# Moving the keys' trailing subtraction of the rotated rows from VectorE to Pool

## The chip, the cores and the metric

One core of one Trainium2 chip runs the whole program: a decoder layer in float32. The time is device microseconds (us) of one launch. Engines: PE is TensorE, DVE is VectorE, ACT is ScalarE, POOL is GpSimd (called Pool in the text), SP is SyncE, which only issues DMAs here.

## The reference

The input x is 4 sequences of 1024 rows of 256 numbers. The layer is self-attention with 16 heads of 16, cross-attention over 77 rows of context, and a mixture of 8 experts. The change touches the projection of the self-attention only:

```python
qkv = x @ qkv_w.T + qkv_b          # x is the layernorm of the input
q = q * cos + x_rot(q) * sin       # apply_rotary
k = k * cos + x_rot(k) * sin
attn = softmax(einsum('bhqd,bhkd->bhqk', q, k) * scale)
```

## The kernel before

The program runs in stages: the projection (`project_qkv`, 0 to some 104 us of the trace), the attention (`attend`), cross-attention and experts.

**Chunks.** The projection takes the 4096 rows in J = 8 chunks of 512, c = 0 to 7; two chunks are one sequence. For each chunk the rows are normalised, transposed, and multiplied by the weights. Products are made of a leading and a trailing part of each float32 number, so that three passes of TensorE give the precision.

**Pairs.** The queries of chunk c are pair n = 2c, the keys are pair n = 2c + 1. One pair goes through these steps, each on one engine:

- TensorE `pair(n)` (L416, L419) multiplies into two banks.
- VectorE `rotate(n)` (L331, twice) multiplies them by the tables into `a_by_even` and `a_by_odd`. It waits until Pool has summed pair n - 2, whose buffers it overwrites.
- Pool (L392) adds the two into `a_rotated`, which has one half for queries and one for keys. Here this is called sum n.
- ScalarE `split(n)` (L263) copies the sum into `a_parts` as the leading part.
- VectorE `split(n)` (L339) subtracts the leading part from the sum; this is the trailing part. Here it is called subtraction n.
- SyncE `store_pair(n)` (L164) stores the parts to `q_stacks` or `k_stacks` with 4 DMAs.

The last three pairs (13, 14, 15) have their subtractions in the next stage, on Pool (`end_sums`, L174 to L180).

**The rest of VectorE's list.** In chunk c it runs `rotate(2c)`, `trailing(c + 1)` (L319, the trailing part of the transposed rows, read from PSUM), `moments(c + 3)` (L302, L305), subtraction 2c - 1, in chunks 0, 2 and 4 `spread(c + 2, 2)`, then `rotate(2c + 1)` and subtraction 2c. `spread` makes one over the standard deviation of the next two chunks in 13 tiny instructions that wait for each other: three TENSOR_SCALAR (L312, L60, L61), nine of Newton's steps (L67, L68, L69) and L314. ScalarE can only normalise chunks c + 2 and c + 3 (L237, `a_xn`) behind it, and TensorE transposes them (L404) behind that.

**The other orders.** ScalarE's list in chunk c is: copy of the values (L254), `take(c + 1)` (L245), leading parts 2c - 1 and 2c, copy of the values, their store (L156), `normalise(c + 2)`. Pool's list is the sums in order, with two memsets (L471, `b_k`, the padding of the first group) between sum 2 and sum 3. SyncE's list is the stores in order of pairs; behind the store of pair 7 and of pair 9 it issues the loads of `b_q` and `b_k` (L483) for the first group of heads, behind the store of pair 11 that of `b_v` (L486), and then the store of pair 12. All the engines meet at a barrier between the projection and the attention.

**The start of the attention.** TensorE's first products there (L879) are for the row maxima; they wait for all of the first group (`pe.wait_ge(s_ld[0], LD)`). VectorE reduces each (L811). The maxima of the first rows go by DMA into `b_q` (L677). The first scores (L930) wait for that, and with them the main loop, which TensorE and VectorE fill. Pool, behind the barrier, does `end_sums`, clears the padding of group 1 and issues its loads; SyncE stores the last three pairs.

Of the kernel before, what the change touches and what calls it, by code (L numbers as in the profile page):

```python
# [8 lines left out]
F32 = mybir.dt.float32  # L9
# [85 lines left out]
def project_qkv(nc, ps, ident, s_id, group0, s_clear0, stores, tail, s_end, cw, x, wts, qst, kst, vst):  # L95
# [5 lines left out]
    with ctx:  # L101
        sb = lambda n, s, d=F32: ctx.enter_context(nc.sbuf_tensor(n, s, d))
        sem = lambda n: ctx.enter_context(nc.semaphore(n))
        J = 2 * B
# [33 lines left out]
        s_eo = sem("a_rotated")  # L138
# [7 lines left out]
        def after(eng, s, n):  # L146

            if n > 0:
                eng.wait_ge(s, n)

        def half(c):
            return slice(CH * (c % 2), CH * (c % 2) + CH)

        def store_v(sp, c):
            i, h = c // 2, c % 2
            sp.dma_start(vst[i][:, NT * h:NT * h + NT, :],  # L156
                         vsb[:, h].rearrange("p t h d -> p t (h d)")).then_inc(s_vs[h], 16)
# [43 lines left out]
        @block.sync  # L201
        def _(sp):
            load(sp, 0)
            sp.dma_start(w, wts["wqkv"]).then_inc(s_w, 16)
            sp.dma_start(ident[:], wts["ident"]).then_inc(s_id, 16)
            load(sp, 1)
            sp.dma_start(bias[:], wts["bqk"]).then_inc(s_tab[0], 16)
            load_tables(sp, 0)
            load(sp, 2)
            load(sp, 3)  # L210
            load_tables(sp, 1)
            sp.dma_start(cw["wp"][:], wts["wp"].rearrange("(k p) n -> p k n", p=P)).then_inc(s_wp, 16)
            sp.dma_start(cw["bp"][:], wts["bp"].partition_broadcast(P)).then_inc(s_wp, 16)
            sp.dma_start(bv[:], wts["bvqkv"]).then_inc(s_wp, 16)
            for c in range(J - 1):
                sp.wait_ge(s_pb, 2 * c + 1)
                store_pair(sp, 2 * c)
                if c == J - 2:
                    continue
                sp.wait_ge(s_pb, 2 * c + 2)  # L220
                store_pair(sp, 2 * c + 1)
                if c == J - 5:
                    for h in range(2):
                        sp.wait_ge(s_vs[h], 16)
                        sp.wait_ge(s_qs[h], 128)
                    sp.wait_ge(s_clear0, 4)
                if J - 5 <= c < J - 2:
                    load_group(sp, *group0, qst, kst, vst, 0, 0, part=c - J + 5)

        @block.scalar  # L230
        def _(act):
            def normalise(c):
                h = c % 2
                act.wait_ge(s_stat, c + 1 if c < 2 else 2 + c // 2)
                after(act, s_xT, c - 1)
                for t in range(NT):
                    last = nc.scalar.activation(xn[:, h, t, :], xin[:, c % NX, t, :], ACT.Identity,  # L237
                                                bias=nm[:, c % NX, t:t + 1], scale=rs[:, c % NX, t:t + 1])
                last.then_inc(s_xn, 1)

            def take(c):
                act.wait_ge(s_xT, c + 1)
                after(act, s_vp, 2 * c - 2)
                for k in range(KC):
                    last = nc.scalar.activation(xh[:, c % 2, k, :], ps[:, k, :], ACT.Copy)  # L245
                last.then_inc(s_xh, 1)

            def copy_v(m):
                c, u = m // 2, m % 2
                act.wait_ge(s_vp, m + 1)  # L250
                if u == 0:
                    act.wait_ge(s_v0, 1)
                    after(act, s_vs[c % 2], 16 * (c // 2))
                nc.scalar.activation(vsb[:, c % 2, 2 * u:2 * u + 2, :, 0:D],  # L254
                                     ps[:, 6 + u, :].rearrange("p (t h d) -> p t h d", t=2, d=D), ACT.Copy).then_inc(s_vc, 1)

            def split(n):
                c, s = n // 2, n % 2
                act.wait_ge(s_eo, n + 1)
                if s == 0:  # L260
                    after(act, s_qs[c % 2], 128 * (c // 2))
                summed = whole(n, 1).bitcast(F32) if n == 2 * J - 3 else eo[:, n % 2]
                nc.scalar.activation(whole(n, 0), summed, ACT.Copy).then_inc(s_pa, 1)  # L263

            def refill(c):
                if c < J:
                    act.wait_ge(s_xn, c - NX + 1)
                    load(act, c)

            act.wait_ge(s_w, 16)  # L270
            nc.scalar.activation(wh[:], w, ACT.Copy).then_inc(s_wh, 1)
            normalise(0)
            refill(NX)
            take(0)
            normalise(1)
            refill(NX + 1)
            for c in range(J):
                copy_v(2 * c)
                if c + 1 < J:
                    take(c + 1)  # L280
                if c:
                    split(2 * c - 1)
                if c < J - 1:
                    split(2 * c)
                copy_v(2 * c + 1)
                act.wait_ge(s_vc, 2 * c + 2)
                store_v(act, c)
                if c + 2 < J:
                    normalise(c + 2)
                    refill(c + 2 + NX)  # L290

        @block.vector
        def _(dve):
# [27 lines left out]

            def rotate(n):
                q, at = n % 2, half(n // 2)
                after(dve, s_eo, n - 1)
                if n == 2 * J - 1:
                    by = last_even[:], last_sum[:]
                else:
                    by = by_even[:, q], by_odd[:, q]
                for u, s in ((0, s_ev), (1, s_od)):
                    dve.wait_ge(s, n + 1)  # L330
                    last = v.scalar_tensor_tensor(by[u], ps[:, 2 + 2 * q + u, :].unsqueeze(1).to_broadcast([P, 2, CH]),  # L331
                                                  bias[:, 2 * q + u:2 * q + u + 1], tab[:, 2 * u:2 * u + 2, at],
                                                  ALU.add, ALU.mult)
                last.then_inc(s_t, 1)

            def split(n):
                c, s = n // 2, n % 2
                dve.wait_ge(s_pa, n + 1)
                v.tensor_tensor(whole(n, 1), eo[:, n % 2], whole(n, 0).bitcast(F32), ALU.subtract).then_inc(s_pb, 1)  # L339

# [8 lines left out]
            for c in range(J):  # L349
# [6 lines left out]
                    trailing(c + 1)  # L356
                if c and c + 3 < J:
                    moments(c + 3)
                if 0 < c < J - 1:
                    split(2 * c - 1)  # L360
                if c % 2 == 0 and c + 2 < J:
                    spread(c + 2, 2)
                if c == 3:
# [11 lines left out]
        def _(pool):  # L375
            g = nc.gpsimd
            clear_pad(g, pool, group0[0], s_clear0, 0)
            for n in range(2 * J - 1):
                q = n % 2
                after(pool, s_eo, n)  # L380
                if n == 3:
                    clear_pad(g, pool, group0[1], s_clear0, 2)
                pool.wait_ge(s_t, n + 1)
                after(pool, s_pb, n - 1)
                if n == 2 * J - 2:
                    to = sum_before[:]
                elif n == 2 * J - 3:
# [2 lines left out]
                else:  # L390
                    to = eo[:, q]
                g.tensor_tensor(to, by_even[:, q], by_odd[:, q], ALU.add).then_inc(s_eo, 1)  # L392

        @block.tensor
        def _(pe):
# [1708 lines left out]
```

## Time and profile before

| what | value |
|---|---|
| median of 3 runs | 1180.93 us (1179.43 to 1181.35) |
| the profiled execution, its own time | 1183.38 us |
| its span in the trace | 1181.6 us |
| busy PE, DVE, ACT, POOL | 92%, 86%, 65%, 30% of the span |
| projection | 0 to some 104 us |
| first maximum product, first score of the attention | 104.00 us, 137.43 us |

Busy time says how long an engine had work, and not who was waited for. So the questions are put to the stretch of the projection and the start of the attention alone: who idles there, and what ends each wait. Times below are from the start of the span.

### The profile page before, as it was taken

What the parts mean: (1) busy time and instruction counts of PE and PEld (TensorE: products, weight loads), DVE (VectorE), ACT (ScalarE), POOL (GpSimd) and SP (SyncE); (2) the same over time, 40 slices, a digit from 0 to 9 for tenths busy, and PEclk for the clock granted to TensorE, in tenths of its full rate; (3) what the DMA queues carried; (4) which work ended last, traced back from release to release, by engine and by line L of the source; (5) the groups of instructions that cost most, each with busy time, mean ns of one, the idle gap of its engine ahead of it and who ended that gap; (6) DMA issues with size and microseconds to landing.
All of it is one profiled execution on the core that took longest, in us unless ns stands there. A gap on an engine that the chain in (4) does not pass through costs nothing. (4 is left out here: it accounts for less than half of the span.)

```text
span 1181.6 us, 22857 instructions
## 1 busy us (share of the span) xinstructions
PE 1082.7 (92%) x8540; PEld 596.6 (50%) x8540; DVE 1014.3 (86%) x2168; ACT 767.8 (65%) x932; POOL 352.3 (30%) x316
## 2 busy tenths in 40 slices
PE   7989899999999999999999999999984059999998
PEld 6776333333333333333333333347773048888897
DVE  7998799999999999999999999716998975766663
ACT  4552288788888888888887888864565014655653
POOL 2647822202220221122022000022100022765675
PEclk8987599999999999999999999999997559999999
DMA  7787844514422441443144000036532022554443
GB/s 232 258 252 220 199 74 90 97 23 80 75 52 44 80 78 27 69 79 67 24 84 75 20 12 17 17 105 212 178 107 94 0 72 60 152 147 125 111 112 36
DMA packets 84681, 113.95 MB, mean 96 GB/s; under 512 B 25056, under 2 KB 57568, under 8 KB 84576
## 3 DMA queue, kind: packets, MB, share of 16 engines
q1 hardware_dynamic: 66256, 69.82, 20.0%
q0 software_dynamic: 15024, 36.17, 17.0%
q10 hardware_dynamic: 3296, 6.56, 1.6%
q8 instruction: 65, 1.06, 0.4%
q14 instruction: 40, 0.33, 0.1%
HBM read 73.31 MB, written 38.27 MB: 94 GB/s over the span
## 5 line engine op out<-in xcount | busy, mean ns | idle before, releaser
L811 DVE TENSOR_REDUCE b_max_halves<-banks 128x1 f32<-128x512 f32 x1024 | 626.5, 681 | 13.1 <-PE banks L879 12.9
L748 ACT ACTIVATE b_probs<-banks 128x1024 f32<-128x1024 f32 x512 | 520.4, 1026 | 145.3 <-PE banks L930 145.3
L879 PE MATMUL banks<-b_k,b_q 62*128 62x512 f32 x1024 | 398.4, 469 | 6.0 <-PEq L101 1.5
L930 PE MATMUL banks<-b_q,b_k 64*128 64x512 f32 x1024 | 385.6, 456 | 4.5 <-issue 3.3
L901 PE MATMUL banks<-b_probs,b_v 128*17 128x256 f32 (+1 forms) x3840 | 314.8, 400 | 0.2 <-ACT b_probs L748 0.2
L930 PEld LDWEIGHTS banks<-b_q,b_k 64*128 64x128 f32 x1024 | 157.0, 185 | 224.5 <-issue 170.8
L879 PEld LDWEIGHTS banks<-b_k,b_q 62*128 62x128 f32 x1024 | 161.9, 190 | 40.3 <-DVE b_max_halves L811 38.0
L901 PEld LDWEIGHTS banks<-b_probs,b_v 128*17 128x17 f32 x3840 | 63.9, 95 | 165.1 <-issue 98.5
L551 POOL TENSOR_TENSOR b_att<-b_out,b_rec_spread 128x512 f32<-128x512 f32 x32 | 41.1, 1283 | 310.9 <-DMA b_rec_spread<-reciprocals 310.7
L483 POOL DMA_DIRECT2D b_q<-q_stacks x60 | 31.7, 532 | 226.4 <-PE banks L901 214.3
L1850 DVE TENSOR_TENSOR e_hTl<-e_hT,e_hTh 128x512 fp32r<-128x512 f32 x64 | 47.6, 744 | 48.8 <-ACT e_hT L1604 48.8
L1630 POOL DMA_INDIRECT e_x<-rows,d_idx x32 | 45.3, 1414 | 111.0 <-DVE d_wx L1805 57.5
L1601 ACT ACTIVATE e_hTh<-banks,e_b 128x512 fp32r<-128x512 f32 x64 | 44.1, 689 | 52.5 <-PE banks L1962 49.0
L1962 PE MATMUL banks<-e_w2h,e_hTh 128*128 128x256 f32 x256 | 73.1, 286 | 0.0
L1962 PE MATMUL banks<-e_w2l,e_hTh 128*128 128x256 f32 x256 | 72.4, 283 | 0.0
L1962 PE MATMUL banks<-e_w2h,e_hTl 128*128 128x256 f32 x256 | 72.4, 283 | 0.0
L1587 ACT ACTIVATE e_xTh<-banks 128x512 fp32r<-128x512 f32 x16 | 8.7, 596 | 83.3 <-PE banks L1950 83.3
L1653 POOL DMA_INDIRECT out_x<-c_x,d_idx x32 | 55.3, 1728 | 17.7 <-DVE c_x L1883 11.0
L1962 PE MATMUL banks<-e_xTh,e_w1h 128*128 128x512 f32 x128 | 53.9, 421 | 3.2 <-DVE e_xTl L1818 2.6
L1962 PE MATMUL banks<-e_xTl,e_w1h 128*128 128x512 f32 x128 | 51.2, 400 | 0.0
L1962 PE MATMUL banks<-e_xTh,e_w1l 128*128 128x512 f32 x128 | 50.9, 397 | 0.0
L392 POOL TENSOR_TENSOR a_rotated<-a_by_even,a_by_odd 128x1024 f32<-128x1024 f32 x13 | 36.4, 2802 | 47.2 <-DVE a_by_odd L331 46.8
(259 smaller groups left out, 1476.5 us busy)
## 6 DMA issues: line engine op xcount, KB each, us to landing
e_w<-in_w SPq DMA_DIRECT2D x16, 1024.0 KB
q_stacks<-a_parts SPq DMA_DIRECT2D x32, 256.0 KB, 4.2
k_stacks<-a_parts SPq DMA_DIRECT2D x32, 256.0 KB, 4.1
b_q<-q_stacks POOLq DMA_DIRECT2D x30, 256.0 KB, 6.4
b_k<-k_stacks POOLq DMA_DIRECT2D x30, 256.0 KB, 7.2
v_tiles<-a_v ACTq DMA_DIRECT2D x8, 544.0 KB, 3.7
b_rec_spread<-reciprocals SPq DMA_DIRECT2D x128, 32.0 KB, 1.8
attended<-b_att SPq DMA_DIRECT2D x128, 32.0 KB, 2.6
```

The source lines that it names most:

```text
L392: g.tensor_tensor(to, by_even[:, q], by_odd[:, q], ALU.add).then_inc(s_eo, 1)
L551: g.tensor_tensor(self.att[:, x, :], self.osb[:, x, :], self.rb[:, x, :], ALU.mult).then_inc(self.s_att, 1)
L748: nc.scalar.activation(pr[:, S % NP, u], ps[:, 2 * u:2 * u + 2, :], ACT.Exp, scale=D ** -0.5).then_inc(s_ex[u], 1)
L811: v.tensor_reduce(mxp[:, (k // NB) % 2, s, p, t, kh:kh + 1], ps[:, bank(last), :], AX.X, ALU.max)\
L879: nc.tensor.matmul(ps[:, bank(last), :], qs[g][stack, p, at:at + P], ks[g][stack, p, CH * kh:CH * kh + CH], start=True, stop=True).then_in ...
L901: last = nc.tensor.matmul(ps[VW * j:VW * j + VS, PV, at], vs[hg // 2][:, kt, j, :], pr[:, S % NP, j // 2, j % 2, at], start=(kt == 0), sto ...
L930: return nc.tensor.matmul(ps[:, 2 * u + s, :], ks[g][stack, u, P * kt:P * kt + P], qs[g][stack, u, CH * h:CH * h + CH], start=True, stop=True)
L1601: nc.scalar.activation(hh[:, f, :], ps[:, UP[f % len(UP)], :], ACT.Gelu, bias=b1[:, x, f:f + 1])
L1630: g.indirect_dma_start(xe[:, x, h, :], None, xrow, bass.IndirectOffsetOnAxis(ap=idx[:, n, h:h + 1], axis=0))\
L1653: g.indirect_dma_start(out, bass.IndirectOffsetOnAxis(ap=idx[:, n, h:h + 1], axis=0), y[:, h, :], None, compute_op=ALU.add).then_inc(s_sc, 16)
L1850: v.tensor_tensor(hl[:, f, :], hf[:, f % NH, :], hh[:, f, :], ALU.subtract).then_inc(s_hl, 1)
L1962: ins = mm(o, a, b, start=(start and m == 0), stop=(stop and m == len(pairs) - 1))
```

## The change

The keys' subtractions 1, 3, 5, 7, 9 and 11 leave VectorE's list. Pool does each of them behind the sum of the pair that follows: sum 2, subtraction 1, (the memsets), sum 3, sum 4, subtraction 3, and so on. Both operands and the result are the same tiles as before. The queries' subtractions 0, 2, ... 12 stay on VectorE. As Pool's semaphore `s_eo` now counts sums and subtractions, the helper `added(n)` tells its value behind sum n and `parted(n)` its value behind subtraction n; the waits of SyncE, ScalarE and VectorE are rewritten for that.

```diff
@@ -151,6 +151,12 @@
         def half(c):
             return slice(CH * (c % 2), CH * (c % 2) + CH)
 
+        def added(n):
+            return n + 1 + max(0, n // 2 - (n % 2 == 0))
+
+        def parted(n):
+            return added(n + 1) + 1
+
         def store_v(sp, c):
             i, h = c // 2, c % 2
             sp.dma_start(vst[i][:, NT * h:NT * h + NT, :],
@@ -213,11 +219,11 @@
             sp.dma_start(cw["bp"][:], wts["bp"].partition_broadcast(P)).then_inc(s_wp, 16)
             sp.dma_start(bv[:], wts["bvqkv"]).then_inc(s_wp, 16)
             for c in range(J - 1):
-                sp.wait_ge(s_pb, 2 * c + 1)
+                sp.wait_ge(s_pb, c + 1)
                 store_pair(sp, 2 * c)
                 if c == J - 2:
                     continue
-                sp.wait_ge(s_pb, 2 * c + 2)
+                sp.wait_ge(s_eo, parted(2 * c + 1))
                 store_pair(sp, 2 * c + 1)
                 if c == J - 5:
                     for h in range(2):
@@ -256,7 +262,7 @@
 
             def split(n):
                 c, s = n // 2, n % 2
-                act.wait_ge(s_eo, n + 1)
+                act.wait_ge(s_eo, added(n))
                 if s == 0:
                     after(act, s_qs[c % 2], 128 * (c // 2))
                 summed = whole(n, 1).bitcast(F32) if n == 2 * J - 3 else eo[:, n % 2]
@@ -321,7 +327,8 @@
 
             def rotate(n):
                 q, at = n % 2, half(n // 2)
-                after(dve, s_eo, n - 1)
+                if n > 1:
+                    dve.wait_ge(s_eo, added(n - 2))
                 if n == 2 * J - 1:
                     by = last_even[:], last_sum[:]
                 else:
@@ -334,7 +341,6 @@
                 last.then_inc(s_t, 1)
 
             def split(n):
-                c, s = n // 2, n % 2
                 dve.wait_ge(s_pa, n + 1)
                 v.tensor_tensor(whole(n, 1), eo[:, n % 2], whole(n, 0).bitcast(F32), ALU.subtract).then_inc(s_pb, 1)
 
@@ -356,8 +362,6 @@
                     trailing(c + 1)
                 if c and c + 3 < J:
                     moments(c + 3)
-                if 0 < c < J - 1:
-                    split(2 * c - 1)
                 if c % 2 == 0 and c + 2 < J:
                     spread(c + 2, 2)
                 if c == 3:
@@ -377,11 +381,13 @@
             clear_pad(g, pool, group0[0], s_clear0, 0)
             for n in range(2 * J - 1):
                 q = n % 2
-                after(pool, s_eo, n)
+                if n:
+                    pool.wait_ge(s_eo, added(n) - 1)
                 if n == 3:
                     clear_pad(g, pool, group0[1], s_clear0, 2)
                 pool.wait_ge(s_t, n + 1)
-                after(pool, s_pb, n - 1)
+                if n > 1 and q == 0:
+                    pool.wait_ge(s_pb, n // 2)
                 if n == 2 * J - 2:
                     to = sum_before[:]
                 elif n == 2 * J - 3:
@@ -390,6 +396,10 @@
                 else:
                     to = eo[:, q]
                 g.tensor_tensor(to, by_even[:, q], by_odd[:, q], ALU.add).then_inc(s_eo, 1)
+                if q == 0 and 0 < n < 2 * J - 2:
+                    pool.wait_ge(s_pa, n)
+                    pool.wait_ge(s_eo, added(n))
+                    g.tensor_tensor(whole(n - 1, 1), eo[:, 1], whole(n - 1, 0).bitcast(F32), ALU.subtract).then_inc(s_eo, 1)
 
         @block.tensor
         def _(pe):
```

Pool's list, from sum 2 to sum 5. Before:

```order
L392 TENSOR_TENSOR a_rotated<-a_by_even,a_by_odd 128x1024 [waits a_trailing_part,a_parts_of_rotation_ready,a_rotated]
L471 MEMSET b_k 32x2048 [waits a_rotated]
L471 MEMSET b_k 32x2048 [waits group0_pad_cleared]
L392 TENSOR_TENSOR a_rotated<-a_by_even,a_by_odd 128x1024 [waits a_trailing_part,a_parts_of_rotation_ready,group0_pad_cleared]
L392 TENSOR_TENSOR a_rotated<-a_by_even,a_by_odd 128x1024 [waits a_trailing_part,a_parts_of_rotation_ready,a_rotated] x9
```

With the change:

```order
L398 TENSOR_TENSOR a_rotated<-a_by_even,a_by_odd 128x1024 [waits a_trailing_part,a_parts_of_rotation_ready,a_rotated]
L402 TENSOR_TENSOR a_parts<-a_rotated,a_parts 128x2x512 [waits a_rotated,a_leading_part]
L481 MEMSET b_k 32x2048 [waits a_rotated]
L481 MEMSET b_k 32x2048 [waits group0_pad_cleared]
L398 TENSOR_TENSOR a_rotated<-a_by_even,a_by_odd 128x1024 [waits a_parts_of_rotation_ready,group0_pad_cleared]
L398 TENSOR_TENSOR a_rotated<-a_by_even,a_by_odd 128x1024 [waits a_trailing_part,a_parts_of_rotation_ready,a_rotated]
L402 TENSOR_TENSOR a_parts<-a_rotated,a_parts 128x2x512 [waits a_rotated,a_leading_part]
L398 TENSOR_TENSOR a_rotated<-a_by_even,a_by_odd 128x1024 [waits a_parts_of_rotation_ready,a_rotated]
```

A subtraction (now L402) stands behind every sum of queries, and the one in front of the memsets is ahead of sum 3.

VectorE's list in chunk 2, from the rotation of its queries to the first instructions of `spread`. Before:

```order
L331 SCALAR_TENSOR_TENSOR a_by_even<-banks,a_bias,a_cos_sin 128x1024
L331 SCALAR_TENSOR_TENSOR a_by_odd<-banks,a_bias,a_cos_sin 128x1024
L319 TENSOR_TENSOR a_xnT_trailing<-banks,a_xnT_leading 128x512 x2
L302 BN_STATS a_st<-a_x 128x6 x4
L305 BN_AGGR a_mv<-a_st 128x2 x4
L339 TENSOR_TENSOR a_parts<-a_rotated,a_parts 128x2x512
L312 TENSOR_SCALAR a_ve<-a_mv 128x8
L60 TENSOR_SCALAR a_tm<-a_ve 128x8
```

With the change:

```order
L338 SCALAR_TENSOR_TENSOR a_by_even<-banks,a_bias,a_cos_sin 128x1024
L338 SCALAR_TENSOR_TENSOR a_by_odd<-banks,a_bias,a_cos_sin 128x1024
L325 TENSOR_TENSOR a_xnT_trailing<-banks,a_xnT_leading 128x512 x2
L308 BN_STATS a_st<-a_x 128x6 x4
L311 BN_AGGR a_mv<-a_st 128x2 x4
L318 TENSOR_SCALAR a_ve<-a_mv 128x8
L60 TENSOR_SCALAR a_tm<-a_ve 128x8
```

The subtraction between the moments and `spread` is gone; nothing else moved on this engine.

## Rows read from the trace of the kernel before

**Rows 1.** Windows of 10 us: each engine's busy time (x instructions), PEclk, DMA share, GB/s.

```profile
70.00:80.00 10.00, 7.09 (x33) 6.08 (x33) 9.56 (x21) 5.28 (x10) 3.40 (x2) 0.75 0.82 226
...
80.00:90.00 10.00, 10.00 (x57) 8.77 (x56) 9.22 (x8) 5.95 (x10) 6.14 (x3) 0.91 0.96 282
...
90.00:100.00 10.00, 10.00 (x56) 8.69 (x55) 9.09 (x10) 4.29 (x6) 6.14 (x3) 1.00 1.03 286
```

**Rows 2.** Timeline of VectorE, chunks 2 to 5 (start us, us, instruction, idle before).

```profile
50.67 0.17 DVE L314 SCALAR_TENSOR_TENSOR a_nm<-a_mv,a_rs 128x8 f32<-128x8 f32 x1
...
64.65 1.28 DVE L331 SCALAR_TENSOR_TENSOR a_by_even<-banks,a_bias,a_cos_sin 128x1024 f32<-128x1024 f32 x1
...
70.07 1.23 DVE L339 TENSOR_TENSOR a_parts<-a_rotated,a_parts 128x1024 fp32r<-128x1024 f32 x1
...
71.21 0.17 DVE L312 TENSOR_SCALAR a_ve<-a_mv 128x8 f32<-128x8 f32 x1
...
71.82 0.17 DVE L67 SCALAR_TENSOR_TENSOR a_tm<-a_rs,a_ve 128x8 f32<-128x8 f32 x1
...
73.63 0.17 DVE L314 SCALAR_TENSOR_TENSOR a_nm<-a_mv,a_rs 128x8 f32<-128x8 f32 x1
...
80.82 2.49 DVE L339 TENSOR_TENSOR a_parts<-a_rotated,a_parts 128x1024 fp32r<-128x1024 f32 x1
```

**Rows 3.** Timeline of Pool, the same columns.

```profile
36.67 3.68 POOL L471 MEMSET b_k<- 32x2048 f32 x2
...
44.28 2.42 POOL L392 TENSOR_TENSOR a_rotated<-a_by_even,a_by_odd 128x1024 f32<-128x1024 f32 x1 [0.26 <-DVE a_by_odd L331]
...
67.25 2.42 POOL L392 TENSOR_TENSOR a_rotated<-a_by_even,a_by_odd 128x1024 f32<-128x1024 f32 x1 [0.25 <-DVE a_by_odd L331]
...
79.85 2.38 POOL L392 TENSOR_TENSOR a_rotated<-a_by_even,a_by_odd 128x1024 f32<-128x1024 f32 x1 [0.28 <-DVE a_by_odd L331]
...
103.96 0.52 POOL L763 MEMSET b_minus<- 2x512 f32 x1 [2.67 <-POOLq L101]
...
106.97 2.36 POOL L176 TENSOR_TENSOR a_parts<-a_parts 128x1024 fp32r<-128x1024 f32 x1
```

**Rows 4.** Timeline of a later stage: a sum on Pool, small instructions of VectorE.

```profile
833.48 2.35 POOL L1178 TENSOR_TENSOR c_xb<-c_x,c_bp 128x1024 f32<-128x1024 f32 x1 [9.82 <-DMA c_x<-in_x]
...
835.23 0.70 DVE L1283 SCALAR_TENSOR_TENSOR c_ve<-c_mv,c_eps 128x4 f32<-128x4 f32 x2
```

**Rows 5.** Timeline of TensorE, and of VectorE's last maxima ahead of the first score.

```profile
53.00 1.09 PE L404 MATMUL banks<-ident,a_xn 128*128 128x128 f32 x8 [2.65 <-ACT a_xn L237]
...
75.95 1.97 PE L404 MATMUL banks<-ident,a_xn 128*128 128x128 f32 x8 [2.91 <-ACT a_xn L237]
...
104.00 0.70 PE L879 MATMUL banks<-b_k,b_q 62*128 62x512 f32 x3 [1.45 <-PEq L101]
...
125.46 9.66 DVE L811 TENSOR_REDUCE b_max_halves<-banks 128x1 f32<-128x512 f32 x16
...
137.43 0.76 PE L930 MATMUL banks<-b_q,b_k 64*128 64x512 f32 x1 [3.26 <-issue]
```

**Rows 6.** Timeline of DMA issues: SyncE's queue, then ScalarE's last one.

```profile
83.34 2.45 SPq L164 DMA_DIRECT2D k_stacks<-a_parts  x4
...
96.67 0.88 SPq L486 DMA_DIRECT2D b_v<-v_tiles  x1
...
97.59 4.89 SPq L164 DMA_DIRECT2D q_stacks<-a_parts  x4
...
103.21 0.33 ACTq L156 DMA_DIRECT2D v_tiles<-a_v  x1
```

**Rows 7.** Waits from 83 to 108 us: who waited, for whom, us in total, times, longest.

```profile
PEld banks L879 <- DMA b_v<-v_tiles: 1.6, 1, 1.6
```

**Rows 8.** Windows of 2 us, columns as in the first group.

```profile
84.00:86.00 2.00, 2.00 (x10) 1.64 (x9) 2.00 (x3) 1.52 (x3) 0.17 (x1) 1.00 0.83 252
...
130.00:132.00 2.00, 2.00 (x4) 0.94 (x4) 2.00 (x4) 0.00 (x0) 1.94 (x2) 0.50 1.04 175
```

## The prediction

> **What bounds the kernel now.** The chain of the page covers only the end of the program, so I read the windows first. In the projection VectorE is busy 9.56 and 9.22 us of 10, while TensorE is at 7.09 once, with its clock on 0.75, that is half of that stretch at 1.2 and half at 2.4 GHz [rows 1]. So VectorE paces this stage, and an engine with room, Pool (3.40 and 6.14 us of 10), takes work from it. That speaks for a gain. The reader should then see three things against it. TensorE waits 2.65 and 2.91 us for the normalised rows before the transposes of chunks 4 and 6 [rows 5]; these wait for `spread`, which ends on VectorE at 50.84 and 73.80 [rows 2]. The DMA share is 0.96 and 1.03 from 80 to 100 us [rows 1]: the DMAs are full. And at the end TensorE does not start the attention when it has finished; its weight loads wait 1.6 us for the DMA of `b_v` [rows 7], the first product runs at 104.00 [rows 5].
>
> **Does Pool hold VectorE up?** Sum 10 runs on Pool from 79.85 to 82.23 [rows 3], and the subtraction that VectorE begins at 80.82 beside it takes 2.49 us instead of 1.23 [rows 2]. In a later stage even tiny ones wait: two 128x4 instructions (L1283) take 0.70 us when they begin at 835.23 beside a sum of Pool that ends at 835.83, and end 0.1 us behind it [rows 4]; an instruction of that size takes 0.17 [rows 2]. Both kinds read two operands in SBUF, and Pool reads there too. L67, L68, L69 and L314 in `spread` are of that kind. Rotations, `trailing` and moments are not (their inputs are one in PSUM, or one alone), so I let them run.
>
> **The change, step by step.** Six subtractions leave VectorE. An undisturbed one holds it 71.21 - 70.07 = 1.14 us [rows 2], number 9 holds it 2.42. Read as busy time that is 5 x 1.14 + 2.42 = 8.1 us (number 11 taken as undisturbed). Pool gains six of 2.36 us [rows 3]; I lay them into its list and go through the chunks.
>
> - Chunk 1: subtraction 1 is gone, VectorE is 1.14 ahead.
> - Chunk 2: a second 1.14 is gone, but Pool is late. Sum 2 ended at 36.62, and the memsets took its place at 36.67 for 3.68 us [rows 3]. Now subtraction 1 runs first, to 39.05, the memsets to 42.8, sum 3 to 45.25, sum 4 to 47.7 (it began at 44.28 before and is 1.0 later), subtraction 3 to 50.1. `spread` takes 1.81 us from L67 at 71.82 to L314 at 73.63, nine steps of 0.2 [rows 2]; so L67 stood at 50.67 - 1.81 = 48.86 here and would now stand 2.28 earlier, at 46.6. It waits for sum 4 until 47.7, its second step for subtraction 3 until 50.1. Eight steps of 0.2 and the 0.17 of L314 follow. That ends at 51.85 against 50.84: **1.0 us later**. TensorE's wait of 2.65 becomes 3.7.
> - Chunk 3: no `spread`, 1.14 ahead. The rotation at 64.65 starts at some 64.5, **0.1 ahead**.
> - Chunk 4: sum 8 (67.25 to 69.67 before) ends 0.1 earlier, subtraction 7 behind it at 71.95. The first Newton step, ready at 71.82 - 1.14 - 0.1 = 70.6, waits for it; then 1.81 + 0.17 make 73.9 against 73.80. **0.1 late**: the 1.14 removed is paid back by the wait.
> - Chunk 5: VectorE saves the 2.42. But rotation 11 then waits for TensorE's pair 11, and TensorE has worked without a gap since 75.95, so its end does not move by it.
> - Chunk 6: subtraction 11 is removed too. It is covered by the same TensorE work.
>
> So VectorE's path to the transposes ends where it did, and **TensorE's end moves by 0.1 us at most**. Its clock: in the longer wait of chunk 4 it may fall to 1.2 GHz. The slow stretch between 75 and 82 cost some 3.4 us of TensorE's work (0.25 and 0.09 of 10 us at full speed [rows 1]); at chunk 4 such a loss is covered by TensorE's wait before chunk 6, so I cost it at nothing; if the wait before chunk 6, now 2.0 instead of 2.9 us, no longer makes it fall, TensorE ends up to 3.4 us earlier. Neither decides, because of the next step.
>
> - The keys' stores: store 9 is issued at 83.34, as soon as VectorE has finished at 83.31 [rows 2, 6]. Now it waits for Pool: sum 10 ends at 82.3, and 2.36 us of subtraction 9 give 84.7. **1.35 us later.** From there to 102.48 SyncE issues with no gap, and the DMAs have no room to catch up: share 0.83 in the two us in which this store begins [rows 8] and about 1 behind them [rows 1]. So `b_v` (issued at 96.67, landed for 104.00) lands at 105.3, and the last store's issue, 97.59 + 4.89 = 102.48, ends at 103.83 [rows 6]. Stores 1 to 7 get 0.7 to 1.9 us later as well, where the queue has gaps, and cost nothing. Store 11 needs subtraction 11, at 94.1, and its turn comes at 94.4.
> - The barrier: ScalarE's issue ended last, 103.21 + 0.33 = 103.54. Now SyncE's ends last, 103.83. **0.3 us later**; Pool's first memset moves from 103.96 to 104.25 [rows 3].
> - The first maxima start at 105.3, 1.3 late. But VectorE is done with them at 125.46 + 9.66 = 135.12, 2.3 us ahead of the first score at 137.43, before which TensorE idles 3.26 us [rows 5], while the loads that Pool issues behind the barrier hold the DMAs at 1.04 [rows 8]. The rows of maxima land when these loads are through, so I let the first score move with the barrier, 0.3, and not with the maxima, 1.35. Both ends stay for the range.
>
> **Sum**: 1183.38 + 0.3 = 1183.7 us for the profiled execution. It lies 2.45 above the median, 1180.93, so the forecast is **1181.2 us**.
>
> In the Trainium skill, SBUF — State Buffer, section "Who interferes with whom", says that `tensor_scalar` can enter a mode with both read ports and then contends with Pool too. No row here shows that: the profile has no L60 beside a sum. By that rule L312, L60 and L61 would wait as well and run behind subtraction 7, some 0.6 us more in chunk 4, and the forecast would be 1181.8. I go by the rows, where only instructions with two operands in SBUF are seen to wait.
>
> **Rivals.** One, no collision in `spread` (faster): the Newton steps slip through or Pool waits for them. For it: the steps are 0.2 us apart and take 0.17, so Pool could slip in between. Against it: L1283. Then VectorE gains 1.14 in each of chunks 1 to 4, 4.6 us in all, subtraction 9 ends at 80.1 instead of 84.7, and store 9 is up to 3.2 us early; the DMAs have room for most of that, not for all: 1180.93 - 2.7 = **1178.2 us**.
>
> Two, VectorE alone sets the pace and the queue follows: all 8.1 us come through, **1172.8 us**. Against it speak the full DMAs and TensorE, which has no gap from 75.95 on.
>
> Three, the keys' stores set the pace (slower): the DMAs' delay reaches the main loop whole. That is 1.35 us, 1182.3. If subtraction 11 is late too, so that store 11 is issued after 95.6 instead of 94.4, another 1.2 joins it: **1183.5 us**. It decides from the point at which the first maximum product starts after 105.5 and the first score after 138.8. For it: 2.3 us of cover are thin, and Pool gets its work in a lump. Against it: SyncE reaches store 11 only at 94.4.
>
> **How the numbers follow.** A measurement of this kernel can tell 0.2%, 2.4 us, from no change. The forecast (the gain cancelled by waits) has 0.75; the first rival 0.10; the second 0.03; the third 0.12, of which 0.05 is beyond 2.4 us. So faster 0.10 (two thirds of the first rival, and the second), slower 0.05, same 0.85. The range goes from 1178.8, between forecast and first rival, to 1183.0, which holds the 1.35 and the 0.6 us, and leaves out 0.15 or so.
>
> **What would show it.** In the profile of the changed kernel: L67 or its neighbours in chunks 2 and 4 with a duration of 1 to 2.4 us; the end of the second `spread` at 51.9 and of the third at 73.9; store 9 issued at 84.7; rotation 10 within 0.3 us of 77.24; the first maximum product at 105.3, the first score at 137.7. I would be wrong if no small instruction is stretched, if the transposes of chunk 6 start before 75, or if the DMAs make up the delay before 104.

## The result, and the profile after

| | before | changed |
|---|---|---|
| median of the runs taken side by side (8 each) | 1180.72 us | 1184.91 us |
| lowest to highest | 1178.84 to 1183.88 | 1183.24 to 1187.83 |
| the profiled execution, own time / span | 1183.38 / 1181.6 | 1183.72 / 1181.9 |

The ratio is 1.0039, 95% interval 1.0027 to 1.0052: the change costs some 4.6 us (3.2 to 6.1). I had forecast 1181.2 with the range 1178.8 to 1183.0, and slower by over 0.2% with a chance of 0.05. **The prediction was wrong**: slower instead of no change, and outside the range. The profiled execution of the changed kernel is the second fastest of its runs, so it shows where time goes better than how much. One profile shows one execution: where no edit reached, two of them still differ by some 1 us at the end of the projection (TensorE's work there ends 82.4 us behind rotation 0 in the kernel before, 81.4 in e4, whose engines are untouched).

The two profiles do not begin alike. Before, TensorE ran its first work at 1.2 GHz for longer, and the rotation of pair 0 started at 20.13; in the changed kernel it started at 18.52, with no edit ahead of it. So below I count **from rotation 0**: the time in a trace less the start of its rotation 0.

Six subtractions have left VectorE. Its busy time from 20 to 100 us, first before, then changed:

```profile
20.00:100.00 80.00, 73.40 (x418) 64.08 (x418) 76.61 (x140) 42.99 (x68) 44.42 (x17) 0.96 0.79 241
```

```profile
20.00:100.00 80.00, 71.25 (x399) 62.19 (x398) 76.42 (x132) 42.05 (x67) 57.91 (x23) 0.94 0.76 232
```

The third pair of numbers is VectorE's (busy, instructions): 8 fewer (six subtractions and, at the edges, two rotations), the same busy time. The fifth is Pool's: 6 more, 13.5 us more. TensorE, the first, lost 2.15 us. VectorE's timeline shows what filled the place (columns as in [rows 2]):

```profile
18.52 1.28 DVE L338 SCALAR_TENSOR_TENSOR a_by_even<-banks,a_bias,a_cos_sin 128x1024 f32<-128x1024 f32 x1
...
44.49 1.77 DVE L318 TENSOR_SCALAR a_ve<-a_mv 128x8 f32<-128x8 f32 x1
46.29 0.17 DVE L60 TENSOR_SCALAR a_tm<-a_ve 128x8 int32<-128x8 int32 x1
46.50 2.31 DVE L61 TENSOR_SCALAR a_rs<-a_tm 128x8 int32<-128x8 int32 x1
48.84 0.17 DVE L67 SCALAR_TENSOR_TENSOR a_tm<-a_rs,a_ve 128x8 f32<-128x8 f32 x1
...
50.65 0.17 DVE L320 SCALAR_TENSOR_TENSOR a_nm<-a_mv,a_rs 128x8 f32<-128x8 f32 x1
...
57.84 1.40 DVE L308 BATCH_NORM_STATS2 a_st<-a_x 128x6 f32<-128x256 f32 x4
...
59.69 2.35 DVE L369 COPY a_bias_v_spread<-a_bias_v 128x128 f32<-128x128 f32 x2
...
70.89 2.17 DVE L318 TENSOR_SCALAR a_ve<-a_mv 128x8 f32<-128x8 f32 x1
...
75.31 0.17 DVE L320 SCALAR_TENSOR_TENSOR a_nm<-a_mv,a_rs 128x8 f32<-128x8 f32 x1
...
78.92 1.28 DVE L338 SCALAR_TENSOR_TENSOR a_by_even<-banks,a_bias,a_cos_sin 128x1024 f32<-128x1024 f32 x1
...
85.07 2.50 DVE L345 TENSOR_TENSOR a_parts<-a_rotated,a_parts 128x1024 fp32r<-128x1024 f32 x1
...
126.15 9.66 DVE L821 TENSOR_REDUCE b_max_halves<-banks 128x1 f32<-128x512 f32 x16
```

The copy of the bias (L369) was short in the kernel before:

```profile
60.86 0.36 DVE L365 COPY a_bias_v_spread<-a_bias_v 128x128 f32<-128x128 f32 x2
```

And Pool's timeline in the changed kernel:

```profile
37.61 3.66 POOL L481 MEMSET b_k<- 32x2048 f32 x2
41.35 4.88 POOL L398 TENSOR_TENSOR a_rotated<-a_by_even,a_by_odd 128x1024 f32<-128x1024 f32 x2
46.38 2.40 POOL L402 TENSOR_TENSOR a_parts<-a_rotated,a_parts 128x1024 fp32r<-128x1024 f32 x1
...
59.41 2.41 POOL L402 TENSOR_TENSOR a_parts<-a_rotated,a_parts 128x1024 fp32r<-128x1024 f32 x1
...
70.62 2.41 POOL L402 TENSOR_TENSOR a_parts<-a_rotated,a_parts 128x1024 fp32r<-128x1024 f32 x1
...
84.08 2.40 POOL L402 TENSOR_TENSOR a_parts<-a_rotated,a_parts 128x1024 fp32r<-128x1024 f32 x1
...
104.55 0.51 POOL L773 MEMSET b_minus<- 2x512 f32 x1 [3.25 <-POOLq L101]
```

Read the two together. The stretched instructions end just behind Pool: L318 at 46.26 and sum 4 at 46.23, L61 at 48.81 and subtraction 3 at 48.78, L318 at 73.06 and subtraction 7 at 73.03. The two COPYs of L369 end at 62.04, 0.22 behind subtraction 5 (61.82), since the second runs after it. L60, started at 46.29, slipped in between two instructions of Pool. **The instructions that wait are TENSOR_SCALAR and COPY**, the kinds I had let run. BATCH_NORM_STATS2 at 57.84, beside Pool's sum of 56.87 to 59.27, took no longer than elsewhere. And the subtraction of pair 10, at 85.07, waits for Pool's subtraction 9 just as number 9 waited for sum 10 before [rows 2].

Then the engines that wait for VectorE, first TensorE, as in [rows 5]:

```profile
52.98 1.97 PE L414 MATMUL banks<-ident,a_xn 128*128 128x128 f32 x8 [4.24 <-ACT a_xn L243]
...
77.64 1.49 PE L414 MATMUL banks<-ident,a_xn 128*128 128x128 f32 x8 [3.61 <-ACT a_xn L243]
...
104.82 0.73 PE L889 MATMUL banks<-b_k,b_q 62*128 62x512 f32 x3 [1.69 <-DMA b_v<-v_tiles]
...
138.59 0.76 PE L940 MATMUL banks<-b_q,b_k 64*128 64x512 f32 x1 [3.73 <-issue]
```

SyncE's queue, as in [rows 6]:

```profile
86.51 2.47 SPq L170 DMA_DIRECT2D k_stacks<-a_parts  x4
...
98.28 0.92 SPq L496 DMA_DIRECT2D b_v<-v_tiles  x1
99.25 3.31 SPq L170 DMA_DIRECT2D q_stacks<-a_parts  x4
```

And the wait for the last load, as in [rows 7]:

```profile
PEld banks L889 <- DMA b_v<-v_tiles: 1.9, 1, 1.9
```

From rotation 0, the third `spread` ended at 73.80 - 20.13 = 53.7 before and ends at 75.48 - 18.52 = 57.0 now, 3.3 later. The waits of 2.65 and 2.91 us [rows 5] have become 4.24 and 3.61. Store 9 is issued at 68.0 instead of 63.2, 4.8 later. The first maximum product comes at 86.3 instead of 83.9 (2.4 later), the first score at 120.1 instead of 117.3 (2.8 later). What is behind the first score is no longer than before (1181.9 - 138.6 = 1043.3 us against 1044.2). So the profiles show 2.8 of the 4.6 us; where the rest lies is not shown.

What made the barrier late can be read as well. Pool's first memset behind it comes 86.0 from rotation 0 instead of 83.8, 2.2 later. SyncE's queue was through at 99.25 + 3.31 = 102.56; the last to end was ScalarE's issue of the values' store, 1.0 us behind TensorE's last work in both profiles:

```profile
103.80 0.33 ACTq L162 DMA_DIRECT2D v_tiles<-a_v  x1
```

TensorE's projection itself ended 84.6 from rotation 0 instead of 82.4. So here the engines set the barrier; the load of `b_v` then holds the first maximum product only 104.82 - 104.55 = 0.27 us behind the memset, where it was 0.04.

### The profile page after: what moved, and what is told of

Read it like the earlier page. It is cut to its first block and busy times, and to the rows that moved or that the text cites. A ratio compares the mean times of both kernels' runs of the same rounds, so it can differ in the third digit from the quotient of the medians.

```text
span 1181.9 us, 22860 instructions
## 1 busy us (share of the span) xinstructions
PE 1081.7 (92%) x8540; PEld 596.4 (50%) x8540; DVE 1019.5 (86%) x2162; ACT 767.8 (65%) x932; POOL 365.8 (31%) x322
## 5 line engine op out<-in xcount | busy, mean ns | idle before, releaser
L1972 PEld LDWEIGHTS banks<-e_w2h,e_hTh 128*128 128x128 f32 x256 | 49.1, 192 | 0.3
```

Source lines behind the costliest of these rows:

```text
L1972: ins = mm(o, a, b, start=(start and m == 0), stop=(stop and m == len(pairs) - 1))
```

## The experiments

**Theories.** A, collisions: VectorE's small instructions wait for Pool's subtractions, and `spread` and the copy of the values' bias are what carries the delay on to TensorE. B, the queue: only the late store of pair 9 counts. C, the clock: the longer wait before chunk 4's transposes makes TensorE fall to 1.2 GHz, and that counts. Each kernel is timed in turn with the kernel before on the same chip; e1, e3, e4 and e6 share their runs of it, and so do e5, e7, e8 and e9 on a second chip, and e10, e11 and e12 on a third.

In these kernels the set of subtractions on Pool is a tuple, and every wait is worked out from it, so any of them can be on either engine (line numbers are some 8 to 12 higher; `...` marks lines left out):

```diff
+        moved = (1, 3, 5, 7, 9, 11)
+
         def added(n):
-            return n + 1 + max(0, n // 2 - (n % 2 == 0))
+            return n + 1 + sum(m < n - 1 for m in moved)
...
+                if 0 < c < J - 1 and 2 * c - 1 not in moved:
+                    split(2 * c - 1)
...
-                if q == 0 and 0 < n < 2 * J - 2:
+                if n - 1 in moved:
```

Two further edits come in several of them. "Copy late" puts the copy of the bias behind `spread` of chunk 4:

```diff
-                if c == 3:
+                if c == 4:
                     for k in range(KC):
                         last = v.tensor_copy(bvb[:, k, :], bv[:, k:k + 1].to_broadcast([P, P]))
```

"Memsets early" takes the two memsets from between sum 2 and sum 3 to the start of Pool's list:

```diff
             clear_pad(g, pool, group0[0], s_clear0, 0)
+            clear_pad(g, pool, group0[1], s_clear0, 2)
...
-                if n == 3:
-                    clear_pad(g, pool, group0[1], s_clear0, 2)
```

All results in one table. Medians are in us, each with that of the kernel before beside it. The last four columns come from the one profile of each kernel: end of the third `spread`, first score (both from rotation 0), TensorE's wait before the transposes of chunk 6 and its clock behind that wait, in GHz (1.2 where at least part of the next 5 us was at 1.2).

| kernel | on Pool | other edit | median / before | ratio, 95% interval | spread | score | wait | clock |
|---|---|---|---|---|---|---|---|---|
| before | none | | | | 53.7 | 117.3 | 2.91 | 1.2 |
| changed | all six | | 1184.91 / 1180.72 | 1.0039 [1.0027, 1.0052] | 57.0 | 120.1 | 3.61 | 1.2 |
| e1 | all six | copy late | 1182.44 / 1180.85 | 1.0010 [1.0001, 1.0019] | 55.0 | 117.5 | 1.09 | 2.4 |
| e3 | 9, 11 | | 1179.84 / 1180.85 | 0.9996 [0.9986, 1.0005] | 53.7 | 116.9 | 2.79 | 1.2 |
| e4 | none | store 9 late | 1182.63 / 1180.85 | 1.0022 [1.0010, 1.0033] | 53.9 | 120.9 | 2.92 | 1.2 |
| e6 | 5 | | 1182.78 / 1180.85 | 1.0015 [1.0006, 1.0024] | 54.6 | 118.6 | 3.60 | 1.2 |
| e5 | 3, 7 | | 1181.36 / 1180.74 | 1.0012 [1.0001, 1.0023] | 55.4 | 117.8 | 2.41 | 2.4 |
| e7 | 1, 5 | copy late, memsets early | 1178.38 / 1180.74 | 0.9985 [0.9977, 0.9994] | 51.4 | 113.4 | 1.65 | 2.4 |
| e8 | all six | copy late, memsets early | 1180.07 / 1180.74 | 0.9993 [0.9984, 1.0002] | 52.9 | 115.9 | 1.99 | 2.4 |
| e9 | none | copy late, memsets early | 1182.04 / 1180.74 | 1.0004 [0.9992, 1.0015] | 53.4 | 117.2 | 2.26 | 2.4 |
| e10 | all six | as e8, Pool waits for `spread` | 1179.47 / 1180.25 | 1.0000 [0.9989, 1.0010] | 49.2 | 113.9 | 0.51 | 2.4 |
| e11 | all six | memsets early | 1183.52 / 1180.25 | 1.0029 [1.0018, 1.0041] | 55.1 | 117.1 | 4.20 | 1.2 |
| e12 | 1, 5, 9, 11 | copy late, memsets early | 1179.12 / 1180.25 | 0.9989 [0.9980, 0.9998] | 51.4 | 115.3 | 1.65 | 2.4 |

The score column does not give the time: the profile of e11 is the fastest of its seven runs and that of e8 the slowest of its twelve, and e11's first score is not late although its ratio is 1.0029. The ratios tell what a kernel costs, the profiles tell which instruction waited.

### e1: the copy away from the collision

> The changed kernel, but the copy of the values' bias (two COPY instructions of VectorE in chunk 3, 2.35 us in the changed profile where it was 0.36) stands behind the spread of chunk 4. Theory A, collisions: VectorE waits in every instruction that uses its second port while Pool adds or subtracts, TENSOR_SCALAR and COPY too, and the delay reaches transposes and stores alike. Then 2 us come back: +1.5 to +2.5 us against the kernel before instead of +4.2, and store 9 is issued some 2 us earlier. Theory B, only the late store of pair 9 matters, by its own 1.3 us: +4 us as the changed kernel, since Pool's order is the same. Theory C, TensorE's clock falls in the longer wait of chunk 4: no change, +4 us, since that wait stays as long.

VectorE's timeline of e1:

```profile
70.54 0.73 DVE L326 TENSOR_SCALAR a_ve<-a_mv 128x8 f32<-128x8 f32 x1
...
73.62 0.35 DVE L379 COPY a_bias_v_spread<-a_bias_v 128x128 f32<-128x128 f32 x2
```

And TensorE's:

```profile
53.17 1.97 PE L424 MATMUL banks<-ident,a_xn 128*128 128x128 f32 x8 [4.30 <-ACT a_xn L251]
...
75.86 1.09 PE L424 MATMUL banks<-ident,a_xn 128*128 128x128 f32 x8 [1.09 <-ACT a_xn L251]
```

The copy is short again, the third `spread` ends 2.0 us earlier than in the changed kernel, and 0.29% of the 0.39% is gone: 1.0039 - 1.0010, with some 0.15% of uncertainty from both intervals. That speaks for A, with the copy as the dearest collision. C falls as the whole cause: in chunk 4 e1 has the same wait (4.30 against 4.24) with the same long transposes behind it, and costs 0.10% (1.2 us; 0.1 to 2.2, where I had expected 1.5 to 2.5).

### e3: only the two that need no small instruction

> Only the subtractions of pairs 9 and 11 are on Pool; there is no spread and no copy beside them. Theory A: no collision of weight, so TensorE as before; store 9 is 1.2 to 1.4 us later by Pool's work: 0 to +1.3 us. Theory B: the store is as late as my prediction had it, and all of it should show: +1.3 us or more, and the first maximum product that much later. Theory C: no longer wait in chunk 4, so 0.

Pairs 9 and 11 have no `spread` and no copy beside them. Store 9 was issued at 64.75 from rotation 0, 1.5 us later than before, which is the delay that I had predicted for it, and the time did not change: 0.9996. A delay of that size on the queue costs nothing that can be measured, so B as I had priced it is not what costs the 0.39%; and the collisions between big subtractions are not it either.

### e4: the store alone, later still

> The kernel before, all subtractions on VectorE; only the store of pair 9 waits also for subtraction 10, so it is issued 3.5 us later (86.8 instead of 83.3). Engines are untouched. Theory A with the store queue as one of two paths: the first maximum product comes 1.5 to 3.5 us later; the time +1 to +3.5 us if the main loop follows it, near 0 if the cover in front of the first score (2.3 us) holds. Theory B: +3 us or more. Theory C: 0.

```diff
                     sp.wait_ge(s_pb, left(2 * c + 1))
+                if c == 4:
+                    sp.wait_ge(s_pb, 11)
                 store_pair(sp, 2 * c + 1)
```

Nothing moves to Pool here (`left` tells the value of `s_pb` behind a subtraction on VectorE); store 9 only waits for subtraction 10 as well. SyncE's queue:

```profile
85.64 2.45 SPq L175 DMA_DIRECT2D k_stacks<-a_parts  x4
...
96.34 8.46 SPq L175 DMA_DIRECT2D q_stacks<-a_parts  x4
```

The store is 85.64 - 18.65 = 67.0 from rotation 0, 3.8 us late, the queue ends at 104.80, and 0.22% is lost. So the queue is a second path to the same end: 1.5 us late is free, 3.8 us late is not. In e4 the queue sets the barrier, which falls at 86.8 from rotation 0. In the changed kernel store 9 is even 4.8 us late, because VectorE's rotation 10 is 3.3 late, but the queue catches up (the last store takes 3.31 us to issue, 8.46 in e4) and ends 1.6 us before ScalarE. So the delay comes onto B's path from the collisions, and in that profile this path adds at most the 0.27 us at the first maximum product.

### e6: the copy's collision alone

> Only the subtraction of pair 5 is on Pool; it runs beside the copy in chunk 3. Theory A: VectorE saves 1.14 us and waits 2.0 in the copy, so everything behind is 0.8 to 0.9 us later: +0.5 to +1.0 us, with the copy at 2.3 us. Theory B: store 9 moves by 0.9, the same size here. Theory C: 0, the wait of chunk 4 is untouched.

VectorE and TensorE of e6:

```profile
58.67 2.37 DVE L379 COPY a_bias_v_spread<-a_bias_v 128x128 f32<-128x128 f32 x2
```

```profile
75.79 1.97 PE L424 MATMUL banks<-ident,a_xn 128*128 128x128 f32 x8 [3.60 <-ACT a_xn L251]
```

One subtraction of 1.14 leaves VectorE, the copy beside it gets 2.0 us longer, and the third `spread` is 0.9 late. The time rises by 0.15% (1.8 us; 0.7 to 2.8), the first score by 1.3 us. A single moved instruction has lost more than it saved; that is A. Store 9 is 1.0 late here too (83.17 - 19.02 = 64.2), which B had counted on as well, but e3 has shown that 1.5 is free. The cost is larger than the 0.5 to 1.0 us that I expected, but its interval holds the net delay of 0.9.

### e5: the two beside `spread`

> Only the subtractions of pairs 3 and 7 are on Pool, the two that run beside a spread. The memsets are not pushed back, since pair 1 stays on VectorE. Theory A, collisions in every instruction with both ports in use, TENSOR_SCALAR among them: VectorE saves 1.14 us each time and waits about 2 us, so the second spread ends 0.8 us and the third 1.6 us later from rotation 0 on: +1.0 to +2.0 us in all. My prediction's rule, only instructions with two operands in SBUF wait: 1.14 saved and 1.2 to 1.3 waited, +0.1 to +0.4 us.

VectorE of e5:

```profile
45.45 2.17 DVE L326 TENSOR_SCALAR a_ve<-a_mv 128x8 f32<-128x8 f32 x1
47.66 0.17 DVE L60 TENSOR_SCALAR a_tm<-a_ve 128x8 int32<-128x8 int32 x1
...
69.37 2.08 DVE L326 TENSOR_SCALAR a_ve<-a_mv 128x8 f32<-128x8 f32 x1
```

Each time the first instruction of `spread` waits for the subtraction to end, and the rest is undisturbed. Each `spread` pays 2 us for the 1.14 that it gained. The third ends 1.7 us late, and the time is 0.12% up (0.01 to 0.23%). The spreads decide between A and my prediction's rule, which had asked for 0.1 to 0.4 us; the time alone would not.

### e7 and e9: only the free ones, and the control

> The two subtractions that need collide with nothing: pairs 1 and 5 are on Pool, the others on VectorE; the bias copy stands behind the spread of chunk 4, and the two memsets of the first group's padding stand at the start of Pool's list, where Pool is idle. Theory A: VectorE keeps both savings of 1.14 us, and the spreads end 1.1 and 2.3 us earlier from rotation 0 on, store 9 is 2 us earlier; TensorE's work behind it gives back part: -1.0 to -2.2 us against the kernel before. If Pool's work delays VectorE by something other than the collisions, 0 or slower.

> The kernel before with the two side edits alone: bias copy behind the spread of chunk 4, memsets at the start of Pool's list; every subtraction on VectorE. Every theory: 0, at most -0.3 us, since the copy's 0.27 us comes behind the spread that the transposes of chunk 6 wait for.

e7 leaves 3 and 7, which meet `spread` on Pool, on VectorE, and 9 and 11 too. It moves only 1 and 5, with the copy out of the way of 5. VectorE and TensorE of e7:

```profile
47.23 0.17 DVE L326 TENSOR_SCALAR a_ve<-a_mv 128x8 f32<-128x8 f32 x1
...
71.43 0.36 DVE L379 COPY a_bias_v_spread<-a_bias_v 128x128 f32<-128x128 f32 x2
```

```profile
51.99 1.09 PE L423 MATMUL banks<-ident,a_xn 128*128 128x128 f32 x8 [1.66 <-ACT a_xn L251]
...
73.68 1.09 PE L423 MATMUL banks<-ident,a_xn 128*128 128x128 f32 x8 [1.65 <-ACT a_xn L251]
```

Of the small instructions none is stretched, the third `spread` ends 2.3 us before that of the kernel before, twice 1.14, and the time falls by 0.15% (2.4 us in the medians, interval 0.06 to 0.23%). The control e9 has the same two edits and nothing on Pool: 1.0004. So the edits alone are worth nothing, and e7's gain over the control, 0.19% with some 0.14% of uncertainty, is that of the two subtractions. e7 is a little faster than the kernel before.

### e8 and e11: all six, with the memsets early

> All six subtractions on Pool as in the changed kernel, with the bias copy behind the spread of chunk 4 and the memsets at the start of Pool's list. Sum 3 and sum 4 are then on time, and in chunk 2 only subtraction 3 collides. Theory A: the second spread ends 2 us earlier than with the memsets in between, the third likewise: 1 to 2.5 us under the kernel with the copy alone moved, so between -1.0 and +0.5 us against the kernel before. If the memsets' place does not matter: +1.2 us, as that one.

> The changed kernel with the memsets alone moved to the start of Pool's list; the bias copy stays in chunk 3. It completes the square of the two side edits. Theory A: sum 3 and 4 are on time, the second spread ends 2 us earlier than in the changed kernel; the copy still waits 2 us: 2 us under the changed kernel, +1.0 to +2.5 us against the kernel before.

e11 is the changed kernel with the memsets early. Its ratio is 0.10% lower, less than the uncertainty of the difference (some 0.17%), and its cost, 3.4 us (2.1 to 4.8), lies above the 1.0 to 2.5 us that I expected, though the interval reaches into them. The third `spread` ends 1.9 us earlier than in the changed kernel. L318's twin takes 2.04 us here, but L61 no longer 2.31, because Pool's subtraction 3 (44.81 to 47.22) has ended when it runs. e8 has the copy late as well and is level with the kernel before, 0.9993. So the copy's place is worth 0.36% from e11 to e8, and 0.29% from the changed kernel to e1. That is 3.4 to 4.3 us for a stall of 2.0. With its interval (1.6 to 5.2 us) the 0.29% can still be 2.0 us, the 0.36% (2.5 to 6.0) hardly; what could make up the rest is below.

### e10: Pool waits instead of VectorE

> All six on Pool, copy and memsets moved, and Pool waits for the end of the spread before subtractions 3 and 7. No instruction of VectorE in a spread can be stretched. Theory A: the spreads end 1.9 and 1.2 us earlier than with all six and no such waits, but sums 5 and 9 and the stores of pairs 3 and 7 come 1.5 to 3 us later: between -1.6 and +0.5 us against the kernel before. If collisions in the spreads cost nothing, the added waits make it slower than with all six and no waits (-0.7 us).

```diff
                 if n - 1 in moved:
                     pool.wait_ge(s_pa, n)
+                    if n - 1 in (3, 7):
+                        pool.wait_ge(s_stat, 4 if n - 1 == 3 else 5)
```

Pool's timeline of e10, and TensorE's:

```profile
47.96 2.39 POOL L413 TENSOR_TENSOR a_parts<-a_rotated,a_parts 128x1024 fp32r<-128x1024 f32 x1 [3.25 <-DVE a_nm L328]
...
68.57 2.39 POOL L413 TENSOR_TENSOR a_parts<-a_rotated,a_parts 128x1024 fp32r<-128x1024 f32 x1 [3.24 <-DVE a_nm L328]
```

```profile
70.61 1.09 PE L425 MATMUL banks<-ident,a_xn 128*128 128x128 f32 x8 [0.51 <-ACT a_xn L251]
```

Pool idles 3.2 us for `spread`, and `spread` ends at 49.2 from rotation 0, 4.5 us before that of the kernel before: here all the removed time is kept. TensorE's wait before chunk 6 has shrunk to 0.51, its projection ends 5.3 us early, then it waits 3.48 us for `b_v`, and the first score is 3.4 us early. This execution took 1178.07, the second fastest of eleven; over all runs the ratio is 1.0000 [0.9989, 1.0010], no better than e8's 0.9993 [0.9984, 1.0002]. So e10 shows that Pool's wait undoes the stretching, and not that it pays. By the times alone my expectation's other case, that collisions in the spreads cost nothing, is not ruled out; e5's ratio speaks against it.

### e12: four of the six

> The kernel with pairs 1 and 5 on Pool, and pairs 9 and 11 as well. Alone, 9 and 11 made no difference. Theory A: TensorE's work bounds the last chunks, so nothing is gained over pairs 1 and 5 alone; store 9 is up to 1.3 us later: -2.4 to -1.0 us against the kernel before. If VectorE's list bounded the end, another 1 to 2 us would come off.

0.9989 [0.9980, 0.9998], not better than e7. Moving 9 and 11 too adds nothing that can be measured, as e3 had shown by itself.

## Why the prediction was wrong, step by step

- **"Does Pool hold VectorE up?" Right that it does; but the waits took more than the gain.** And I divided the instructions wrongly: "only instructions with two operands in SBUF are seen to wait". The trace before had no TENSOR_SCALAR beside a sum, and I took that for leave to let them run. A later stage of it even had a warning that I overlooked: L1742 took 0.51 us beside Pool's L1650 and 0.25 where Pool only issued a DMA. L318 took 1.77 and 2.17 us, L61 2.31. This is the case in which the rule of the Trainium skill, SBUF — State Buffer, section "Who interferes with whom", spoke against my reading: `tensor_scalar`, `copy` and `cast` can enter a mode with both ports and contend with Pool, when their operands allow that mode. The rows of L318, L61 and L369 agree with it. What I had worked out from it was 1181.8, still too low, since I applied it to `spread` of chunk 4 alone and not to the copy of chunk 3.
- **Chunk 2, "1.0 us later".** Measured 50.82 - 18.52 = 32.3 against 30.7, 1.6 later. Pool ended subtraction 3 at 30.3 from rotation 0, where I had 30.0, and behind it all nine Newton steps and L320 followed instead of eight and L314. The term was mis-sized by 0.6.
- **Chunk 3, "no `spread`, 1.14 ahead": the step that failed.** VectorE also copies the bias there (L365 before, L369 now, ahead of rotation 7), which I did not list. It took 2.35 us beside subtraction 5 instead of 0.36. So 1.6 - 1.14 + 2.0 = 2.5 late. The rotation at 64.65 [rows 2], which I moved to 64.5, started 65.47 - 18.52 = 46.95 from rotation 0 against 44.52: 2.4 late. e6 shows that this collision alone costs more than its subtraction gains, and e1 that most of the loss goes with it.
- **Chunk 4, "0.1 late".** 2.4 - 1.14 + 2.0 (L318's wait) = 3.3 late, as measured. The small instruction waited, not the Newton step, so nothing was overlapped. e5, without the copy's collision, shows this term alone: its `spread` is 0.9 late behind chunk 2 and 1.7 behind chunk 4, so 0.8 where I had 0.1.
- **Chunk 5 and 6, "covered by TensorE".** Subtraction 9's 2.42 us are gone, but subtraction 10 now takes 2.50. And TensorE was late itself, since its transposes of chunk 6 start 59.1 from rotation 0 instead of 55.8. Rotation 10, "within 0.3 us of 77.24", is 3.3 late, and "TensorE's end moves by 0.1 us at most" became 2.2. That e3 lost nothing shows the collisions of big subtractions alone to be harmless.
- **"Store 9, 1.35 us later".** The term was right: e3 gave 1.5. In the changed kernel VectorE's 3.3 came on top: 4.8. But it was not the keys' stores that set the pace, as the third rival had it.
- **"The barrier: now SyncE's ends last, 0.3 us later".** ScalarE's issue still ended last, 104.13 against SyncE's 102.56, and the barrier came 2.2 us later with TensorE's end. This is where the engine delay that I had put at 0.1 entered the time.
- **"I let the first score move with the barrier, 0.3, and not with the maxima, 1.35".** The cover of 2.3 us is not borne out, nor is it refuted. From first maximum product to first score the thirteen profiles take 31.9 to 34.0 us, with the first maximum product up to 4.0 us late (e4) or 3.5 early (e7); from the barrier, read as Pool's first memset, they take 33.1 to 35.0. Where the two part, the profiles disagree: e12 has e7's barrier (80.3 from rotation 0), maxima 1.7 us later and a score 1.9 later; e1 has e11's barrier (83.9), maxima 1.3 later and a score only 0.3 later. So the runs don't say which of the two the score follows. In the changed kernel both were late, 2.2 and 2.4 us.
- **TensorE's clock.** I had said that it may fall in the longer wait of chunk 4, and it did: over 51 to 58 us the granted clock was 0.52, before it had been 1.00. e1 has nearly the same (0.59) and cost 1.2 us in all, its collisions included, so costing it at nothing was nearly right there.

What was never shown is how the loss splits up behind the copy. Windows of 4 us of the changed kernel, then of e1 (columns as in [rows 1]):

```profile
78.00:82.00 4.00, 4.00 (x15) 3.35 (x14) 4.00 (x5) 1.86 (x4) 3.71 (x2) 0.57 1.07 197
```

```profile
78.00:82.00 4.00, 4.00 (x25) 3.52 (x24) 4.00 (x5) 1.14 (x2) 3.75 (x2) 1.00 1.01 166
```

With the clock on 0.57 TensorE does 15 products in 4 us, at full clock 25. In the thirteen profiles the waits of 2.79 us and longer before chunk 6 were followed by a stretch at 1.2 GHz, those of 2.41 and shorter were not. That could add to what the copy's 2.0 us cost. It is argued, not shown, and two things speak against it. The kernel before had the slow stretch too, and the control e9, at 2.4 GHz there, has its first score at 117.2 against 117.3 and the same time. And the length of the wait does not decide alone: before chunk 4 waits of 2.38 and 2.39 us (e11, e8) were followed by 1.2 GHz, one of 2.65 was in e3 and not in e4 or e6. There is one profile for each kernel, so what the loss is made of beyond the late transposes stays open.

## What to carry to other kernels

Before you move work to Pool, list every instruction of VectorE that will stand beside it, single copies too, with its operands. Beside a sum or subtraction on Pool, TENSOR_SCALAR, COPY and the instructions with two operands in SBUF waited here until it ended, however small they were. A move paid where VectorE read PSUM or took moments meanwhile (e7, 0.15%); where a chain of tiny instructions is due, leave the work on VectorE. To let Pool wait for the chain (e10) kept the chain short, but no gain in time was measured. And a kind of instruction that the trace does not show beside Pool has no price yet: bound it by the dear case, not by the free one.

## What the hardware showed that I had not expected

- A COPY of two 128x128 tiles, 0.36 us by itself, took 2.35 and 2.37 beside one 128x1024 subtraction of 2.41 on Pool. A TENSOR_SCALAR of 128x8 took up to 2.31 instead of 0.17. VectorE's rotations (1.28) and BATCH_NORM_STATS2 (1.40 for four) were not longer beside Pool.
- The wait lasts until the Pool instruction ends, but between two of them VectorE gets its turn: L60 ran in 0.17 us at 46.29, between sum 4 and subtraction 3, and L61 behind it lost 2.1.
- VectorE holds Pool up as well: in e6 the sum that starts at 52.33 beside VectorE's subtraction of 52.11 to 53.32 takes 3.27 us, the next, with rotations beside it, 2.42.
- Not all work on Pool holds VectorE. In the kernel before, the subtraction at 37.02 took 1.23 us, as undisturbed, though Pool's memsets ran beside it from 36.67 to 40.35. And beside Pool's TENSOR_SCALAR of a later stage a TENSOR_SCALAR of VectorE got longer, but ended at 1031.10 while Pool's two ran on to 1032.68 (spans on Pool are rough):

```profile
956.61 0.25 DVE L1742 TENSOR_SCALAR d_rv<-d_hi,d_pid 128x128 bf16<-128x128 bf16 x1
...
1029.87 2.81 POOL L1650 TENSOR_SCALAR c_x<-c_x,d_wx 128x256 f32<-128x256 f32 x2
1030.59 0.51 DVE L1742 TENSOR_SCALAR d_rv<-d_hi,d_pid 128x128 bf16<-128x128 bf16 x1
```
